# Cross-attention on one core: joins of the maxima ahead of the block maxima, K out behind the scores, and two products moved to GpSimd

## The chip, the core and the metric

The kernel runs on one core of one Trainium2 chip. A core has five engines that run their own queues in order and wait for each other by semaphores: PE (TensorE, matrix products, results into PSUM banks), ACT (ScalarE), DVE (VectorE), POOL (GpSimd, no access to PSUM) and SP (SyncE, which issues most DMAs here). The metric is the device time of one execution in microseconds (us); lower is better.

## What is computed

Layer norm of a context, multi-head cross-attention over it, an output projection with a gate and a residual, for 32 batches of 112 queries and 375 context rows, 512 features, 16 heads of 32, all in float32:

```python
a = _layer_norm(audio_kv, ln_gamma, ln_beta)
Q = (hidden_states @ Wq.T).reshape(B, Tt, HEADS, HEAD_DIM).transpose(0, 2, 1, 3)
K = (a @ Wk.T).reshape(B, Ta, HEADS, HEAD_DIM).transpose(0, 2, 1, 3)
V = (a @ Wv.T).reshape(B, Ta, HEADS, HEAD_DIM).transpose(0, 2, 1, 3)
scores = jnp.einsum('bhtd,bhsd->bhts', Q, K) * scale
scores = jnp.where(mask, scores, jnp.float32(-jnp.inf))
attn = jax.nn.softmax(scores, axis=-1)
out = jnp.einsum('bhts,bhsd->bhtd', attn, V)
out = out.transpose(0, 2, 1, 3).reshape(B, Tt, D)
out = out @ Wo.T
return hidden_states + jnp.tanh(gate) * out
```

## The kernel before

**Split products.** Each large product is made of three passes: both factors are split into a high part, which TensorE's fast float32 format holds exactly, and a low part (the rest), and high·high, high·low and low·high are added. So for each tensor there is a high half (a copy into that format, on ACT for the context and the attention output) and a low half (a subtraction of the high half).

**Stages.** In the first 92 us the weights are prepared, all of Q is computed (L960) and kept in DRAM. Then the main loop runs over 64 slot pairs m. A slot, or chunk, p is a group of four heads of one batch: 4 per batch, 128 in all. Slot pair m belongs to batch c = m // 2 and is even or odd. In what follows "slot" with a number up to 63 means such a pair.

**PE in slot m.** K projection of chunk 2m, a V part (or, in odd slots from batch 3 on, the output product of batch c − 3 as the fourth product), K projection of chunk 2m+1, another of these; the weighted sums of chunks 2m−6 and 2m−5 (L1093) with their denominators (L1099); and the scores of chunks 2m and 2m+1 (L1080). K projections all use bank KB = 6, as do the weighted sums; V and outputs use bank 7. The scores of a chunk have three parts j of 125 context rows. The two chunks of a slot share banks 0 to 5: parts 0 and 1 of the even chunk lie in banks 0 to 3, part 2 begins in banks 4 and 5.

**The maxima.** After ACT has moved the scores to `prob` (L608, scaled, with the mask as bias), DVE takes block maxima over 32 rows by transposing reductions (L833, `quadrant_maxima`), three for each chunk. They are in four partition quarters; SP stores them to DRAM and loads them back so that each partition has all of them (`exchange_maxima`, L361 and L368, into `x4` for even chunks, `x_odd` for odd ones). One slot later DVE joins them (L821, into `top`), spreads the result over the columns of PSUM bank 0 (L824, `spread`), and subtracts it from the scores (L843, three times). ACT takes the exponential (L617), POOL adds the three parts of a chunk (L475, L479, `sum_chunks`), and the denominators are made of these sums. In the last but one pair the spread maxima lie in SBUF, in `rspread`, instead of the bank.

**Normalising and output.** ACT moves the weighted sums and denominators out (L658, `weighted_out`). Once per batch, in even slots, DVE reduces the denominators, takes the reciprocal, spreads it into `rspread` and multiplies (`normalise`, L848 to L858). In the odd slot behind it ACT makes the high half (L634), DVE the low half (L862). PE multiplies by Wo one batch later, ACT moves this out with the gate (L640, `gated`), POOL adds the input with its bias (L461, L467), SP stores.

**What sets the order.** Every engine's queue is written by hand in a function `slot_pair(m)` of its own, and what follows the loop stands behind it. The last batch is drained separately: the weighted sums of chunks 122, 124 and then 126 and 127, outputs 29, 30 and the last, which is split into quarters (`last_divide`, `last_low`, `last_output`). The semaphores named in the change are `sub_done` (subtractions), `o_norm` (a batch is normalised), `o_hi` and `o_done` (its high and low halves), `rspread_done` and `top_done`.

## Time and profile before

| what | value |
|---|---|
| median of 3 runs | 960.72 us (960.67 to 962.39) |
| the profiled execution | 958.61 us |
| its span, first to last instruction | 956.8 us |
| mean granted TensorE clock | 0.996 |
| PE busy | 932.9 us, 97% |
| DVE busy | 810.9 us, 85% |
| ACT busy | 689.6 us, 72% |
| POOL busy | 589.6 us, 62% |

The page is read from the busy shares to the waits: an engine that is busy throughout sets the pace, and idle time of the others costs nothing unless it ends in a wait of that engine. Busy times are those of instructions as the profiler records them; the ends of matmuls are modelled. A row of a timeline shows instructions of one kind merged; the bracket at its end is the idle time of that engine before them and what ended it.

### The profile page before, as it was taken

The page shows a single profiled execution, that of the slowest core. Times are in us where ns is not written, and L with a number is a line of the kernel's source. Part 1 is how long each engine was busy: PE and PEld are TensorE (multiplying, and loading weights), DVE is VectorE, ACT ScalarE, POOL GpSimd, SP SyncE. Part 2 cuts the span into 40 slices and gives each one's busy share as a digit, 9 for nine tenths or more (in the row PEclk, how much of TensorE's full clock was granted, in tenths as well). Part 3 has the DMA queues.
Part 4 walks back from the last instruction along what each step waited for, and adds up shares of the span by engine and source line. Part 5 has one row for each costly group of instructions (what it writes and reads, how often), then busy time and mean ns, then how long its engine had stood idle before and what let it go on. Part 6 is the DMA issues. An engine that isn't in the chain of part 4 may idle for free.

```text
span 956.8 us, 26687 instructions
## 1 busy us (share of the span) xinstructions
PE 932.9 (97%) x10687; PEld 807.7 (84%) x10687; DVE 810.9 (85%) x1446; ACT 689.6 (72%) x1299; POOL 589.6 (62%) x665
## 2 busy tenths in 40 slices
PE   8999988999999999999999999999999999999967
PEld 8889877888888888888888888888888888888854
DVE  6873379898888899889988888898889988888896
ACT  2422677777877778777778787778777778777773
POOL 0851356666666667766667666667676667666554
PEclk9999999999999999999999999999999999999999
DMA  9974133324443333444344444334444344433101
GB/s 284 348 223 166 28 94 93 93 70 108 108 113 101 97 93 98 110 112 106 95 98 112 110 105 105 85 94 113 109 112 109 80 110 109 113 94 99 38 21 58
DMA packets 85852, 105.54 MB, mean 110 GB/s; under 512 B 22529, under 2 KB 63489, under 8 KB 85729
## 3 DMA queue, kind: packets, MB, share of 16 engines
q1 hardware_dynamic: 85152, 102.93, 40.5%
q8 instruction: 84, 1.38, 0.6%
q10 hardware_dynamic: 576, 0.92, 0.3%
q14 instruction: 40, 0.32, 0.1%
HBM read 86.39 MB, written 17.43 MB: 109 GB/s over the span
## 4 chain that ended last, share of the span: by engine, by line
PE 88%; DVE 6%; DMA 2%; POOL 1%; ACT 1%; issue 1%; SPq 0%; DVEq 0%; ACTq 0%; POOLq 0%
PE banks L937 62%; PE banks L1080 10%; PE banks L1093 8%; PE banks L960 5%; PE banks L1099 2%; DVE shared_q L843 2%; DMA shared_q<-in_wvT 2%; DVE rmax L833 1%; DVE banks L824 1%; POOL gbo L445 1%; POOL xy L449 1%; ACT shared_q L608 1%; DMA shared_q<-in_wqT 0%; DVE top L821 0%; DVE wq L737 0%
## 5 line engine op out<-in xcount | busy, mean ns | idle before, releaser
L937 PE MATMUL banks<-shared_r,w_k 128*128 128x376 f32 x1536 | 291.7, 339 | 0.0
L937 PE MATMUL banks<-w_v,shared_r 128*125 128x512 f32 x1152 | 284.4, 396 | 0.0
L937 PEld LDWEIGHTS banks<-shared_r,w_k 128*128 128x128 f32 x1536 | 263.1, 188 | 12.9
L475 POOL TENSOR_TENSOR shared_f<-shared_q 125x448 f32<-125x448 f32 x126 | 146.9, 1166 | 199.6 <-PE banks L1099 198.4
L833 DVE TRANSPOSE_TENSOR_REDUCE rmax<-shared_q 128x14 f32<-128x448 f32 x384 | 220.6, 620 | 55.5 <-ACT shared_q L608 55.4
L608 ACT ACTIVATE shared_q<-banks,maskT,rstd 125x448 f32<-125x448 f32 x384 | 249.9, 726 | 4.8 <-PE banks L1080 4.8
L937 PEld LDWEIGHTS banks<-w_v,shared_r 128*125 128x125 f32 x1152 | 213.2, 186 | 45.2 <-issue 0.2
L843 DVE TENSOR_TENSOR shared_q<-shared_q,banks 125x448 f32<-125x448 f32 x378 | 212.0, 616 | 4.4
L617 ACT ACTIVATE shared_q<-shared_q 125x448 f32<-125x448 f32 x384 | 193.1, 569 | 5.9 <-DVE shared_q L843 5.8
L479 POOL TENSOR_TENSOR shared_f<-shared_f,shared_q 125x448 f32<-125x448 f32 x126 | 154.0, 1222 | 9.9
L455 POOL TENSOR_TENSOR shared_r<-cn,shared_r 128x375 fp32r<-128x375 f32 x124 | 111.9, 923 | 75.1 <-ACT shared_r L564 75.0
L628 ACT ACTIVATE shared_f<-banks,rstd 125x512 f32<-125x512 f32 x96 | 66.2, 689 | 60.5 <-PE banks L937 60.5
L1080 PE MATMUL banks<-shared_q,shared_f 32*125 32x112 f32 x3072 | 101.5, 276 | 6.4 <-DVE shared_q L843 6.4
L1080 PEld LDWEIGHTS banks<-shared_q,shared_f 32*125 32x125 f32 x3072 | 90.2, 184 | 18.0 <-issue 18.0
L1093 PEld LDWEIGHTS banks<-shared_q,shared_f 125*32 125x32 f32 x3072 | 72.4, 110 | 32.3 <-issue 23.1
L1093 PE MATMUL banks<-shared_q,shared_f 125*32 125x112 f32 x3072 | 89.0, 263 | 8.0 <-ACT shared_q L608 5.4
L937 PE MATMUL banks<-w_o,shared_r 128*112 128x512 f32 x372 | 91.9, 396 | 0.1
L622 ACT ACTIVATE shared_f<-banks 128x376 f32<-128x376 f32 x128 | 62.3, 487 | 40.9 <-PE banks L937 40.9
L824 DVE STREAM_TRANSPOSE banks<-top 128x448 f32<-128x448 f32 x126 | 83.1, 660 | 4.3
L960 PE MATMUL banks<-shared_r,wq 128*128 128x448 f32 x384 | 82.6, 377 | 0.7 <-ACT wq L546 0.7
L960 PEld LDWEIGHTS banks<-shared_r,wq 128*128 128x128 f32 x384 | 73.6, 192 | 9.1 <-issue 1.0
L937 PEld LDWEIGHTS banks<-w_o,shared_r 128*112 128x112 f32 x372 | 64.5, 174 | 19.0 <-DVE shared_r L862 0.3
(94 smaller groups left out, 742.9 us busy)
## 6 DMA issues: line engine op xcount, KB each, us to landing
cn<-in_ctxT SPq DMA_DIRECT2D x128, 187.5 KB, 3.7
rows<-in_ctx SPq DMA_DIRECT2D x32, 720.0 KB
xy<-in_x SPq DMA_DIRECT2D x32, 224.0 KB, 7.3
q_kept<-shared_q SPq DMA_DIRECT2D x8, 896.0 KB, 5.4
shared_q<-q_kept SPq DMA_DIRECT2D x32, 224.0 KB, 4.3
out<-xy SPq DMA_DIRECT2D x32, 224.0 KB, 3.6
shared_f<-in_xT SPq DMA_DIRECT2D x7, 896.0 KB, 11.0
x<-row_stats SPq DMA_DIRECT2D x64, 84.0 KB
```

Of the source, the lines that this page charges most:

```text
L455: pool.tensor_tensor(cT[:, p, 1, k, 0:S], cn[:, m % (2 * KT), :], cT[:, p, 0, k, 0:S].bitcast(F32), ALU.subtract) \
L475: pool.tensor_tensor(psum[0:SP_, h, :], prob[0:SP_, q, 0, :], prob[0:SP_, q, 1, :], ALU.add).then_inc(sum_half, 1)
L479: pool.tensor_tensor(psum[0:SP_, h, :], psum[0:SP_, h, :], prob[0:SP_, q, 2, :], ALU.add).then_inc(sum_done, 1)
L608: act.activation(prob[0:SP_, n % NB, j, :] .rearrange("p (a h t) -> p a h t", a=2, h=2), score_view(n, j), ACT.Identity, bias=maskT[0:SP_, ...
L617: act.activation(prob[0:SP_, n % NB, j, :], prob[0:SP_, n % NB, j, :], ACT.Exp, scale=SCALE).then_inc(exp_done, 1)
L824: dve.transpose(maxima_of(p).rearrange("p (k a) -> p k a", a=32), top[:, :].unsqueeze(2).to_broadcast([128, BLK, 32])) \
L833: last = dve.tensor_reduce(rmax[:, n % 2, BLK * j:BLK * j + BLK], prob[:, n % NB, j, :].rearrange("p (k a) -> p k a", a=32), AX.X, ALU.max ...
L843: dve.tensor_tensor(prob[0:SP_, p % NB, j, :], prob[0:SP_, p % NB, j, :], maxima_of(p)[0:SP_, :], ALU.subtract).then_inc(sub_done, 1)
L937: last = pe.matmul(dst, l, m, start=(start and k == 0), stop=(stop and k == len(pairs) - 1))
L960: return pe.matmul(q_bank(g, m)[:, 0:GN], wq[:, a, k, 128 * m:128 * m + 128], xr[:, g, c, k, :], start=(k == 0 and e == 0), stop=(k == KT ...
L1080: last = pe.matmul(bank[banks[h]][0:SP_, T * places[h]:T * places[h] + T], kT[part, n % 2, SP_ * j:SP_ * j + SP_], qT[part, c % QB, u, :], ...
L1093: pe.matmul(dst[HD * h:HD * h + HD, :], v_sb[0:SP_, c % VB, j, col:col + HD], prob[0:SP_, p % NB, j, T * h:T * h + T], start=(j == 0), sto ...
```

## The change

- `join_maxima`: the joins of the chunks of slot m−1 are made ahead of the block maxima of slot m, both of them, into a `top` of two halves; then, behind the block maxima, come two spreads and six subtractions.
- The spread maxima lie in bank 4 and bank 5 (even and odd chunk), for the last two chunks in bank 0. PE's wait for the subtractions stands ahead of part 2 of the even chunk's scores instead of ahead of part 0.
- ACT: K out of the even chunk (`k_out(2m+2)`) comes behind both score evictions; the exponential of the odd chunk (`exponential(2m−3)`) ahead of `weighted_out`.
- The product by the reciprocal (`normalised`) and the low half (`low_half`) are POOL's. In the loop they stand behind the sums of the slot, the product in even slots and the low half in odd ones; for batch 30 both stand behind the loop, ahead of the sums of chunks 124 and 125.
- DVE waits for `o_norm` before it writes `rspread` again.

```diff
-        top = sb("top", [128, BLK])
+        top = sb("top", [128, 2, BLK])
...
@@ gpsimd
+            def normalised(b):
+                pool.wait_ge(rspread_done, b + 1)
+                o = pv[:, b % 2 * HT:b % 2 * HT + HT]
+                pool.tensor_tensor(o, o, rspread[:, :], ALU.mult).then_inc(o_norm, 1)
+
+            def low_half(b):
+                pool.wait_ge(o_hi, b + 1)
+                pool.tensor_tensor(oT[:, 1, :, :].rearrange("p c t -> p (c t)"),
+                                   pv[:, b % 2 * HT:b % 2 * HT + HT],
+                                   oT[:, 0, :, :].rearrange("p c t -> p (c t)").bitcast(F32),
+                                   ALU.subtract).then_inc(o_done, 1)
...
                 if pair(m - 2):
                     sum_chunks(2 * m - 4)
                     sum_chunks(2 * m - 3)
+                if odd and c > 1:
+                    low_half(c - 2)
                 if not odd and m >= 0:
+                    if c > 1:
+                        normalised(c - 2)
...
             for m in range(-1, PAIRS):
                 slot_pair(m)
+            normalised(B - 2)
+            low_half(B - 2)
             add_bias(B - 3)
             sum_chunks(SLOTS - KT)
             sum_chunks(SLOTS - KT + 1)
@@ scalar, slot_pair
+                if pair(m - 2):
+                    exponential(2 * m - 3)
                 if pair(m - 3):
                     weighted_out(2 * m - 6)
-                if pair(m - 2):
-                    exponential(2 * m - 3)
...
                 if pair(m):
                     scores_out(2 * m)
-                if pair(m + 1):
-                    k_out(2 * m + 2)
...
                 if pair(m):
                     scores_out(2 * m + 1)
                 if pair(m + 1):
+                    k_out(2 * m + 2)
                     first_out(m + 1)
@@ vector
-                return rspread[:, :] if p // 2 == PAIRS - 2 else spread
+                if p // 2 == PAIRS - 2:
+                    return rspread[:, :]
+                return bank[0 if p // 2 == PAIRS - 1 else 4 + p % 2][:, 0:HT]
...
+                need(dve, o_norm, b)
                 dve.transpose(rspread[:, :].rearrange("p (k a) -> p k a", a=32),
...
-                dve.wait_ge(rspread_done, b + 1)
-                o = pv[:, b % 2 * HT:b % 2 * HT + HT]
-                dve.tensor_tensor(o, o, rspread[:, :], ALU.mult).then_inc(o_norm, 1)
...
+                if pair(m - 1):
+                    join_maxima(2 * m - 2)
+                    join_maxima(2 * m - 1)
                 if m == PAIRS - 1:
+                    dve.wait_ge(o_norm, B - 2)
                     without_maximum(SLOTS - 4)
                     without_maximum(SLOTS - 3)
                 quadrant_maxima(2 * m)
                 quadrant_maxima(2 * m + 1)
                 if pair(m - 1) and m < PAIRS - 1:
-                    without_maximum(2 * m - 2)
-                    without_maximum(2 * m - 1)
+                    spread_maximum(2 * m - 2)
+                    spread_maximum(2 * m - 1)
+                    subtract_maximum(2 * m - 2)
+                    subtract_maximum(2 * m - 1)
@@ tensor, scores
                     need(pe, s_out, n * ST)
-                    need(pe, sub_done, (n - 2) * ST)
                 for j in range(ST):
                     banks, places = score_place(n, j)
+                    if n % 2 == 0 and j == 2:
+                        need(pe, sub_done, (n - 2) * ST)
```

In the rows below a line number of the changed kernel differs from that of the kernel before; the names tell them apart. VectorE (DVE) in an even slot and the start of the odd one, before:

```order
L858 TENSOR_TENSOR shared_f<-shared_f,rspread 128x448 [waits rspread_done]
L833 TENSOR_REDUCE rmax<-shared_q 128x14 [waits s_out,max_stored]
L833 TENSOR_REDUCE rmax<-shared_q 128x14 [waits s_out] x2
L833 TENSOR_REDUCE rmax<-shared_q 128x14 [waits s_out,max_stored]
L833 TENSOR_REDUCE rmax<-shared_q 128x14 [waits s_out] x2
L821 TENSOR_REDUCE top<-x_49 128x14 [waits ld_max0]
L824 STREAM_TRANSPOSE banks<-top 128x448 [waits top_done]
L843 TENSOR_TENSOR shared_q<-shared_q,banks 125x448 [waits spread_done]
L843 TENSOR_TENSOR shared_q<-shared_q,banks 125x448 x2
L821 TENSOR_REDUCE top<-x_odd 128x14 [waits ld_max1]
L824 STREAM_TRANSPOSE banks<-top 128x448 [waits top_done]
```

The same engine after, from the joins on:

```order
L839 TENSOR_REDUCE top<-x_49 128x14 [waits ld_max0]
L839 TENSOR_REDUCE top<-x_odd 128x14 [waits ld_max1]
L853 TENSOR_REDUCE rmax<-shared_q 128x14 [waits s_out,max_stored]
L853 TENSOR_REDUCE rmax<-shared_q 128x14 [waits s_out] x2
L853 TENSOR_REDUCE rmax<-shared_q 128x14 [waits s_out,max_stored]
L853 TENSOR_REDUCE rmax<-shared_q 128x14 [waits s_out] x2
L844 STREAM_TRANSPOSE banks<-top 128x448 [waits top_done] x2
L863 TENSOR_TENSOR shared_q<-shared_q,banks 125x448 [waits spread_done]
```

The two joins (of `x4`, printed `x_49`, and `x_odd`) have moved ahead of the six block maxima, and the product by `rspread` is gone. ScalarE (ACT) in an odd slot, from the gated eviction of the output to K out, before:

```order
L640 ACTIVATE gated<-banks,gat 112x512 [waits y_done,y_mm]
L634 ACTIVATE shared_r<-shared_f 128x448 [waits y_mm,o_norm]
L658 ACTIVATE shared_f<-banks 128x2x224 [waits dsum_done,o_done,pv_mm]
L617 ACTIVATE shared_q<-shared_q 125x448 [waits sub_done] x3
L608 ACTIVATE shared_q<-banks,maskT,rstd 125x448 [waits s_mm]
L608 ACTIVATE shared_q<-banks,maskT,rstd 125x448 x2
L622 ACTIVATE shared_f<-banks 128x376 [waits k_mm]
L608 ACTIVATE shared_q<-banks,maskT,rstd 125x448 [waits s_mm]
L608 ACTIVATE shared_q<-banks,maskT,rstd 125x448 x2
```

The same after:

```order
L657 ACTIVATE gated<-banks,gat 112x512 [waits y_done,y_mm]
L651 ACTIVATE shared_r<-shared_f 128x448 [waits y_mm,o_norm]
L634 ACTIVATE shared_q<-shared_q 125x448 [waits sub_done] x3
L675 ACTIVATE shared_f<-banks 128x2x224 [waits dsum_done,o_done,pv_mm]
L625 ACTIVATE shared_q<-banks,maskT,rstd 125x448 [waits s_mm]
L625 ACTIVATE shared_q<-banks,maskT,rstd 125x448 x2
L625 ACTIVATE shared_q<-banks,maskT,rstd 125x448 [waits s_mm]
L625 ACTIVATE shared_q<-banks,maskT,rstd 125x448 x2
L639 ACTIVATE shared_f<-banks 128x376 [waits k_mm]
```

The exponentials now stand ahead of the eviction of the weighted sums, and K out behind the six score evictions. GpSimd (POOL) at the end of the kernel, from `result(28)` to the end, before:

```order
L467 TENSOR_TENSOR xy<-xy,gated 112x512 [waits y_out,xb_done]
L461 TENSOR_TENSOR xy<-xy,gbo 112x512 [waits ld_x1]
L475 TENSOR_TENSOR shared_f<-shared_q 125x448 [waits pv_mm,exp_done]
L479 TENSOR_TENSOR shared_f<-shared_f,shared_q 125x448 [waits exp_done,sum_half]
L475 TENSOR_TENSOR shared_f<-shared_q 125x448 [waits pv_mm,exp_done]
L479 TENSOR_TENSOR shared_f<-shared_f,shared_q 125x448 [waits exp_done,sum_half]
L467 TENSOR_TENSOR xy<-xy,gated 112x512 [waits y_out,xb_done]
```

The same after:

```order
L466 TENSOR_TENSOR xy<-xy,gated 112x512 [waits y_out,xb_done]
L472 TENSOR_TENSOR shared_f<-shared_f,rspread 128x448 [waits rspread_done]
L476 TENSOR_TENSOR shared_r<-shared_f,shared_r 128x448 [waits o_hi]
L460 TENSOR_TENSOR xy<-xy,gbo 112x512 [waits ld_x1]
L486 TENSOR_TENSOR shared_f<-shared_q 125x448 [waits pv_mm,exp_done]
L490 TENSOR_TENSOR shared_f<-shared_f,shared_q 125x448 [waits exp_done,sum_half]
L486 TENSOR_TENSOR shared_f<-shared_q 125x448 [waits pv_mm,exp_done]
L490 TENSOR_TENSOR shared_f<-shared_f,shared_q 125x448 [waits exp_done,sum_half]
```

The product and the low half of batch 30 (L472, L476) now stand ahead of the bias addition and the sums of chunks 124 and 125.

## Rows read from the trace of the kernel before

**Rows 1.** the page: the span, and TensorE's busy tenths in 40 slices of it
```profile
span 956.8 us, 26687 instructions
...
PE   8999988999999999999999999999999999999967
```

**Rows 2.** waits of PE: operation, releaser, us in total, times, longest us
```profile
PE banks L1080 <- DVE shared_q L843: 6.4, 4, 1.9
```

**Rows 3.** timeline of PE, first slots: start us, us, line, operation, count, [idle before]
```profile
123.46 1.58 PE L1080 MATMUL banks<-shared_q,shared_f 32*125 32x112 f32 x48 [1.06 <-DVE shared_q L843]
...
162.00 1.58 PE L1080 MATMUL banks<-shared_q,shared_f 32*125 32x112 f32 x48 [1.87 <-DVE shared_q L843]
```

**Rows 4.** timeline of SP (DMA issues), same columns: one early, two late
```profile
112.62 0.53 SPq L368 DMA_DIRECT2D x_odd<-row_stats  x1
...
916.42 0.53 SPq L361 DMA_DIRECT2D row_stats<-rmax  x1
919.48 0.52 SPq L368 DMA_DIRECT2D x_odd<-row_stats  x1
```

**Rows 5.** timeline of DVE, a steady pair of slots: product and low half
```profile
413.06 1.61 DVE L858 TENSOR_TENSOR shared_f<-shared_f,rspread 128x448 f32<-128x448 f32 x1
...
423.36 0.63 DVE L862 TENSOR_TENSOR shared_r<-shared_f,shared_r 128x448 fp32r<-128x448 f32 x1
```

**Rows 6.** timeline of ACT, one steady odd slot
```profile
422.18 0.69 ACT L640 ACTIVATE gated<-banks,gat 112x512 f32<-112x512 f32 x1 [0.91 <-PE banks L937]
422.76 0.57 ACT L634 ACTIVATE shared_r<-shared_f 128x448 fp32r<-128x448 f32 x1
423.93 0.54 ACT L658 ACTIVATE shared_f<-banks 128x448 f32<-128x448 f32 x1 [0.59 <-issue]
424.37 1.50 ACT L617 ACTIVATE shared_q<-shared_q 125x448 f32<-125x448 f32 x3
425.77 1.95 ACT L608 ACTIVATE shared_q<-banks,maskT,rstd 125x448 f32<-125x448 f32 x3
```

**Rows 7.** timeline of PE, end of the kernel
```profile
932.32 2.47 PE L1093 MATMUL banks<-shared_q,shared_f 125*32 125x112 f32 x48 [5.39 <-ACT shared_q L608]
...
935.40 3.05 PE L937 MATMUL banks<-w_o,shared_r 128*112 128x512 f32 x12
...
940.84 3.04 PE L937 MATMUL banks<-w_o,shared_r 128*112 128x512 f32 x12
```

**Rows 8.** timeline of PE, the odd slot of rows 6
```profile
422.07 1.36 PE L1093 MATMUL banks<-shared_q,shared_f 125*32 125x112 f32 x48
...
423.74 1.58 PE L1080 MATMUL banks<-shared_q,shared_f 32*125 32x112 f32 x48
425.25 0.96 PE L937 MATMUL banks<-shared_r,w_k 128*128 128x376 f32 x4
```

**Rows 9.** timeline of POOL, the first sum of that slot
```profile
423.80 1.19 POOL L475 TENSOR_TENSOR shared_f<-shared_q 125x448 f32<-125x448 f32 x1 [2.69 <-PE banks L1099]
```

**Rows 10.** timeline of DVE, end of the kernel
```profile
922.82 3.74 DVE L843 TENSOR_TENSOR shared_q<-shared_q,rspread 125x448 f32<-125x448 f32 x3
...
937.14 0.65 DVE L853 STREAM_TRANSPOSE rspread<-rden 128x448 f32<-128x448 f32 x1
...
948.83 0.28 DVE L883 TENSOR_TENSOR shared_r<-shared_f,shared_r 128x112 fp32r<-128x112 f32 x1 [0.17 <-ACT shared_r L645]
949.02 0.85 DVE L876 RECIPROCAL shared_f<-banks 128x112 f32<-128x112 f32 x1
...
953.32 0.75 DVE L891 SCALAR_TENSOR_TENSOR xy<-banks,gat,xy 112x512 f32<-112x512 f32 x1 [0.79 <-PE banks L1061]
```

**Rows 11.** timeline of POOL, end of the kernel
```profile
935.33 1.15 POOL L475 TENSOR_TENSOR shared_f<-shared_q 125x448 f32<-125x448 f32 x1 [7.63 <-PE banks L1099]
```

**Rows 12.** windows: busy us (x) of PE, PEld, DVE, ACT, POOL, PEclk, DMA share, GB/s
```profile
932.00:934.00 2.00, 1.69 (x37) 1.69 (x41) 0.94 (x2) 0.84 (x2) 0.00 (x0) 0.50 0.11 23
```

**Rows 13.** waits of PEld, PE's weight loads, in the columns of rows 2
```profile
PEld banks L1080 <- issue: 18.0, 64, 2.1
```

23 lines of the change are left out of this document (9 added, 14 removed).

## The prediction

> **What bounds the kernel now.** I read the page first: TensorE is at nine tenths or full in every slice except the first ones and the last two of a span of 956.8 us [rows 1]. So in the loop nothing that another engine gives up can shorten the time; only PE's idle places and the drain at the end can move it. I then read the waits of PE. The wait of the score matmuls for the subtraction of the maxima comes only four times, 6.4 us in all [rows 2]. Three of the four are in the first slots, the first 1.06 and the third 1.87 us [rows 3]; with 1.54 for the one between (the total less the other three, to the rounding) they are 4.47; the fourth (1.89) is in the last slot, and there PE soon runs into a longer wait anyway. Once the loop is in step the score matmuls follow the weighted sums with no wait. Last I read the timelines of all engines for one steady pair of slots and for the last 50 us, since the change reorders every queue.
>
> **Start of the loop.** The spread maxima of slots m−1 leave bank 0, so scores of slot m wait for the subtraction only ahead of their third part, which begins about a third into 1.5 us, some 0.5 us later. The joins lie ahead of the block maxima, so some 0.8 us (estimate: two operations shorter than 0.5 each) leave VectorE's queue behind the last of these. The second and third stall (1.54 and 1.87) need about 2 us, and these two steps together with the earlier start of ScalarE's score evictions (K out no longer stands between them, about 0.4 us) cover them: I take both as gone. The first one is doubtful. The odd join now stands ahead of the block maxima, and its load is issued at 112.62 [rows 4]. No row shows a load's landing; the nearest is a store's round trip, from 916.42 to 919.48, 3.06 us with its issue [rows 4]. So the join cannot start before about 115.7. Behind it come six block maxima, two spreads and six subtractions, 14 operations of 448 columns, each at most the 0.63 us of an uncontended one [rows 5]; at 0.57 in a row they end near 123.7 at the latest value of the landing and 123.3 at one 0.4 earlier, and the third part of the scores wants them near 122.9 (123.46 − 1.06 + 0.5). About 0.6 of 1.06 stays. Gain at the start: 4.47 − 0.6 = **3.9 us** (3.2 to 4.5).
>
> **The steady slots.** VectorE gives up the product and the low half; GpSimd takes them. PE's sequence of work is the same, and its own time is what a slot costs. What I have to ask is whether a new wait appears. K out behind all scores: six score evictions, 1.95 us for three with the overlap of a next one [rows 6], take 3.7 us from the end of the scores, and K out less than 0.5. PE's second K projection of the next slot, which needs it, begins some 4.9 us after the end of the scores, behind two products (3.04 us for one of 512 columns, three quarters of that for one of 376 [rows 7]; less what overlaps): 0.6 us to spare. Weighted sums out behind the exponential is tight. In an odd slot PE starts the weighted sums at 422.07 and needs their bank for the next K projection at 425.25 [rows 8]. ScalarE starts the gated eviction at 422.18, the high half 0.58 us later, then another 0.47, then three exponentials that free it after 1.40, then the eviction of 0.54 [rows 6]. 422.18 + 0.58 + 0.47 + 1.40 + 0.54 = 425.17, where it was 423.93 + 0.54 = 424.47. That leaves 0.08 us for a semaphore's hop from ScalarE to PE. The one hop that these rows show, from PE's output product (its successor starts at 422.07) to ScalarE at 422.18, is 0.11 us. So the wait is between nothing (a hop inside the slack) and 0.1 us, in 28 odd slots: 0 to 2.8 us. I take the difference to the hop shown, 0.02 to 0.03 us each, **0.6 us**. The next score evictions, queued behind it on ScalarE, start when the scores end, near 425.4, and are not moved.
>
> GpSimd: the product lasted 1.61 us on VectorE while GpSimd was summing, the low half 0.63 while it was idle [rows 5]; on GpSimd each is priced as its own 448-column sum, 1.15 to 1.19, and before the next sums it sat idle for 2.69 us in that slot [rows 9]. One added operation in each slot fits, so in the loop they cost nothing. The low half is ready some 6 us later, and PE wants it a whole pair of slots on. If that cover were gone each slot would cost up to 1.2 us.
>
> Here the Trainium skill speaks against the move: GPSIMD Engine Reference, section "Engine selection", says to keep elementwise work with two inputs on VectorE because GpSimd is about twice as slow. The uncontended rows agree (1.15 against 0.63). The contended product does not bear it out, 1.61 against 1.15, and by the page's factor of about two on 0.63 the two operations would take 2.5 us together instead of my 2.3; that would add 0.2 us to the drain below and nothing in the loop.
>
> **The drain.** Here the two operations are on the path. The last slot's maxima first: load of the odd maxima was issued at 919.48 [rows 4]. The block maxima end about 0.5 us earlier than before, so the load starts near 919.0, and lands (again by the store's round trip) near 921.7. The join now stands ahead of the even slot's subtraction, so spread and subtraction start near 922.4 to 922.8, where the subtraction started at 922.82 [rows 10]; it runs beside GpSimd's sums as before (3.74 us for three). From there the exponentials and evictions run in the order they had. The fourth stall is thus covered by this chain. Call S the start of the next weighted sums, 932.32 before [rows 7]; I take S = **931.9** (931.1 to 932.4).
>
> Before, from S to the end of VectorE's last operation were 953.32 + 0.75 − 932.32 = 21.75 us [rows 7, 10]. After, follow GpSimd's queue. The spread reciprocal ends at 937.79, S + 5.48 [rows 10], unchanged. GpSimd then has, in this order, the product (to S + 6.7), the low half, which waits for ScalarE's high half (from S + 7.4 to S + 8.55), a bias addition (1.3, by its 512 columns against 448), and only then the four sums for the chunk pair 124 and 125. These started at 935.33, S + 3.0, before [rows 11]; now at S + 9.85. Four of them at 1.15 to 1.19 end at S + 14.6. PE is in order: the denominators of that pair wait, behind them the output product of batch 30, which started at 940.84, S + 8.5 [rows 7], and now starts at S + 15.1. So PE has idled some 7 us but for eight small matmuls. After the 5.39 us idle time the granted clock was 0.50, the level of 1.2 GHz [rows 12], and the work from 932.32 to 935.40 [rows 7] took 3.08 us where the same took 1.67 in the loop [rows 8]. So I charge 1.5 us (0 to 2.1, the whole product at half speed) on 3.05: output 30 ends at S + 19.6.
>
> Behind it everything is serial. ScalarE evicts it (0.62) and only then takes the last three exponentials (1.40) [rows 6], the first high quarter (0.3, as a low one) and VectorE two low quarters (0.28 each, overlapping) [rows 10]: so the third reciprocal starts 2.8 us after output 30. From there to the end were 954.07 − 949.02 = 5.05 us [rows 10], with nothing to shorten them. The end is S + 19.6 + 2.8 + 5.05 = S + 27.4 = 959.3 against 954.07. What the freed VectorE gains (its last subtraction ends some 3.5 us earlier) waits for GpSimd. Drain: **+5.2 us** (+3.1 with a warm clock and S at 931.4, +6.4 with a fully cold product and S at 932.3).
>
> **The sum.** −3.9 + 0.6 + 5.2 = +1.9 us on a span of 956.8. The profiled execution took 958.6 and the median of the runs is 960.7; I add the difference to the median: **962.6 us**, which is 0.2% slower. About 0.2%, 1.9 us, is also what a measurement of this kernel can tell from no change.
>
> **Rivals.**
> (A) ScalarE's margin is gone: the exponential ahead of the eviction makes the K projection wait 0.1 us or more in each odd slot. For it: 0.08 us of slack in [rows 6, 8]. Against: the hop may fit. It decides as soon as hop and jitter exceed 0.08 us. Price 0.1 × 28 = 2.8 instead of 0.6: **964.8**, slower. Chance 0.19.
> (B) A shorter head of the scores, the other side: PE's weight loads sit idle before the 64 score blocks, 18.0 us in all with no releaser [rows 13], and one of its three waits moves to the third part, where it is hidden by running matmuls. If 0.06 us of that is the wait itself, 64 slots give −3.8: **958.8**, faster. Against: the same number of waits is issued, the moved one in the middle of a block of short matmuls. Chance 0.13.
> (C) The drain costs less: warm clock, early load, and all three stalls gone: −4.5 + 0 + 3.1 = −1.4, **959.3**; for it only that three uncertain terms all lie at their good end. Chance 0.08. That the order isn't what it seems is no case: GpSimd's queue has the low half ahead of the sums.
>
> **Chances and range.** My forecast holds 0.60, over 960.4 to 964.2; 0.36 of it within 0.2% of 960.7, 0.24 slower. (A) gives 0.17 slower, 0.02 same; (B) 0.10 faster, 0.03 same; (C) 0.05 faster, 0.03 same. Faster 0.15, same 0.44, slower 0.41. The range goes from 959.1, inside (B) and (C), to 965.6, beyond (A).
>
> **What would show it.** No wait of score matmuls for subtractions after slot 5, and at most one short one before. On GpSimd the four last sums start near 10 us after S. PE idles twice in the drain for GpSimd's sum, then shows a clock of 0.50. The last three exponentials follow the eviction of output 30. In odd slots the K projection's wait for ScalarE is 0 to 0.1 us. I am wrong if those last sums start at S + 3, if PE waits in steady slots for anything longer, or if the slots get shorter or longer without a wait.

## The result and the profile after

The changed kernel takes **966.87 us** (median of 4 runs, 964.51 to 969.5) against 960.69 for the kernel before in the same comparison (959.33 to 962.39): a ratio of 1.0068, with a 95% interval of 1.005 to 1.0086. It is slower by some 6 us. I had forecast 962.6, in a range of 959.1 to 965.6, so the prediction was wrong. It charged the drain and missed a ring through the exchange of the maxima: a chain of waits that leads from the load of one slot's maxima to the load of the next slot's, and so has to fit into one slot.

The page of the kernel after, with its span, TensorE's busy tenths and the engines' shares of the chain that ended last; it answers to [rows 1]:

```profile
span 967.7 us, 26688 instructions
...
PE   8999999999999999999999999999999999999955
...
PE 61%; DMA 22%; DVE 7%; ACT 4%; issue 2%; POOL 2%; SPq 1%; DVEq 0%; ACTq 0%; POOLq 0%
```

The tenths tell little: two early slices are fuller than before, the last two emptier. The last line tells more: 22% of the chain is DMA, in a kernel whose PE is "full" in every slice of the loop. The same line before:

```profile
PE 88%; DVE 6%; DMA 2%; POOL 1%; ACT 1%; issue 1%; SPq 0%; DVEq 0%; ACTq 0%; POOLq 0%
```

Next, PE's waits in the kernel after (operation, releaser, us in total, times, longest), which answer to [rows 2]:

```profile
PE banks L1112 <- ACT shared_q L625: 9.5, 1, 9.5
PE banks L1118 <- POOL shared_f L490: 6.4, 2, 4.7
PE banks L955 <- ACT shared_f L675: 2.0, 6, 0.4
...
PE banks L1099 <- DVE shared_q L863: 1.7, 2, 1.1
```

The first two are in the drain, the third is a K projection that waits for ScalarE's eviction of the weighted sums, the fourth is what is left of the waits for subtractions. VectorE's waits, same columns:

```profile
DVE top L839 <- DMA x_odd<-row_stats: 131.4, 54, 4.1
```

The join of the odd maxima waits for its load in 54 of 64 slots, 131.4 us in all. None of these waits is there before.

**Stages.** For each kernel I cut the profiled execution at starts that all have, and give the length of each stage in us. "Start" runs from the first K projection (after the preparation) to the 10th slot's scores, "loop" from there to those of the 63rd (53 slots), "last" from there to S, the start of the weighted sums of chunk 122, and "drain" to the end of VectorE's last operation. The last column is the median of all timed runs.

| kernel | start | loop | last | drain | sum | median |
|---|---|---|---|---|---|---|
| before | 122.53 | 693.60 | 24.37 | 21.75 | 862.25 | 960.69 |
| after | 121.17 | 696.01 | 24.98 | 28.06 | 870.22 | 966.87 |
| e1_joins_behind | 118.67 | 694.13 | 22.98 | 28.47 | 864.25 | 959.74 |
| e2_last_on_dve | 120.39 | 696.10 | 26.22 | 22.95 | 865.66 | 961.44 |
| e3_act_order_back | 121.42 | 693.59 | 24.99 | 28.04 | 868.04 | 964.02 |
| e4_behind_and_last | 118.68 | 694.13 | 24.05 | 21.85 | 858.71 | 955.19 |
| e5_also_act_back | 118.30 | 693.59 | 24.16 | 22.95 | 859.00 | 955.10 |
| e6_even_join_ahead | 118.53 | 694.68 | 22.80 | 28.41 | 864.42 | 960.12 |
| e7_products_on_dve | 122.65 | 698.36 | 25.70 | 21.75 | 868.46 | 960.71 |
| e8_only_move | 122.20 | 693.60 | 23.64 | 27.49 | 866.93 | 963.60 |
| e9_ring_shorter | 119.04 | 694.55 | 23.62 | 28.68 | 865.89 | 961.57 |
| e10_ring_longer | 119.86 | 694.64 | 25.12 | 28.60 | 868.22 | 963.72 |

The preparation, whose code is the same everywhere, ended between 90.2 and 94.7 us in these executions, so it is left out of the stages. After is 8.0 us longer by the stages: start −1.4, loop +2.4, last +0.6, drain +6.3. The medians differ by 6.2; the profiled execution of before is 2.1 under its median and that of after 2.6 over, of which the preparation explains 2.9. The other 1.8 of the 8.0 belong to these two executions and not to the kernels.

How far one execution can be trusted shows in e2 (below), which has the code of after up to S: its loop agrees to 0.1 us, its start differs by 0.8 and its last stage by 1.2. So small differences of the loop can be read from one execution, those of the start and the last stage only when they are larger than about 1 us.

### The profile page after: what moved, and what is told of

Same layout as the page of the kernel before. It is cut to its first block, busy times and chain, and to the rows that moved or that the text cites. A ratio compares the mean times of both kernels' runs of the same rounds, so it can differ in the third digit from the quotient of the medians.

```text
span 967.7 us, 26688 instructions
## 1 busy us (share of the span) xinstructions
PE 937.1 (97%) x10687; PEld 809.8 (84%) x10687; DVE 705.1 (73%) x1384; ACT 692.4 (72%) x1299; POOL 646.5 (67%) x727
## 4 chain that ended last, share of the span: by engine, by line
PE 61%; DMA 22%; DVE 7%; ACT 4%; issue 2%; POOL 2%; SPq 1%; DVEq 0%; ACTq 0%; POOLq 0%
PE banks L955 42%; DMA row_stats<-rmax 13%; DMA x_odd<-row_stats 8%; PE banks L1099 6%; PE banks L1112 5%; PE banks L978 5%; DVE rmax L853 5%; DMA shared_q<-in_wvT 2%; PE banks L1118 2%; ACT shared_q L634 2%; ACT shared_q L625 2%; SPq L367 1%; POOL gbo L444 1%; POOL xy L448 1%; DVE shared_q L863 1%
## 5 line engine op out<-in xcount | busy, mean ns | idle before, releaser
L625 ACT ACTIVATE shared_q<-banks,maskT,rstd 125x448 f32<-125x448 f32 x384 | 243.4, 728 | 23.8 <-PE banks L1099 23.8
L486 POOL TENSOR_TENSOR shared_f<-shared_q 125x448 f32<-125x448 f32 x126 | 144.6, 1148 | 169.5 <-ACT shared_q L634 110.9
L853 DVE TRANSPOSE_TENSOR_REDUCE rmax<-shared_q 128x14 f32<-128x448 f32 x384 | 209.8, 610 | 17.4 <-ACT shared_q L625 17.4
L634 ACT ACTIVATE shared_q<-shared_q 125x448 f32<-125x448 f32 x384 | 197.4, 570 | 31.6 <-DVE shared_q L863 31.2
L863 DVE TENSOR_TENSOR shared_q<-shared_q,banks 125x448 f32<-125x448 f32 x378 | 204.9, 606 | 0.1
L490 POOL TENSOR_TENSOR shared_f<-shared_f,shared_q 125x448 f32<-125x448 f32 x126 | 144.6, 1148 | 9.9
L839 DVE TENSOR_REDUCE top<-x_odd 128x14 f32<-128x168 f32 x64 | 29.2, 456 | 131.6 <-DMA x_odd<-row_stats 131.4
L955 PE MATMUL banks<-w_o,shared_r 128*112 128x512 f32 x372 | 94.2, 403 | 0.0
```

The lines of the kernel that those rows point to most:

```text
L486: pool.tensor_tensor(psum[0:SP_, h, :], prob[0:SP_, q, 0, :], prob[0:SP_, q, 1, :], ALU.add).then_inc(sum_half, 1)
L490: pool.tensor_tensor(psum[0:SP_, h, :], psum[0:SP_, h, :], prob[0:SP_, q, 2, :], ALU.add).then_inc(sum_done, 1)
L625: act.activation(prob[0:SP_, n % NB, j, :] .rearrange("p (a h t) -> p a h t", a=2, h=2), score_view(n, j), ACT.Identity, bias=maskT[0:SP_, ...
L634: act.activation(prob[0:SP_, n % NB, j, :], prob[0:SP_, n % NB, j, :], ACT.Exp, scale=SCALE).then_inc(exp_done, 1)
L853: last = dve.tensor_reduce(rmax[:, n % 2, BLK * j:BLK * j + BLK], prob[:, n % NB, j, :].rearrange("p (k a) -> p k a", a=32), AX.X, ALU.max ...
L863: dve.tensor_tensor(prob[0:SP_, p % NB, j, :], prob[0:SP_, p % NB, j, :], maxima_of(p)[0:SP_, :], ALU.subtract).then_inc(sub_done, 1)
```

## The ring, in the trace of after

SyncE's timeline over two slots and a half (start us, us to issue, line, transfer):

```profile
558.89 0.52 SPq L367 DMA_DIRECT2D x_odd<-row_stats  x1
...
564.78 0.53 SPq L360 DMA_DIRECT2D row_stats<-rmax  x1
566.91 0.54 SPq L367 DMA_DIRECT2D x<-row_stats  x1
567.55 0.53 SPq L360 DMA_DIRECT2D row_stats<-rmax  x1
570.85 0.52 SPq L367 DMA_DIRECT2D x_odd<-row_stats  x1
571.42 0.94 SPq L275 DMA_DIRECT2D cn<-in_ctxT  x2
572.41 0.83 SPq L281 DMA_DIRECT2D rows<-in_ctx  x2
...
576.86 0.54 SPq L360 DMA_DIRECT2D row_stats<-rmax  x1
580.93 0.55 SPq L367 DMA_DIRECT2D x<-row_stats  x1
...
584.89 0.52 SPq L367 DMA_DIRECT2D x_odd<-row_stats  x1
```

The ring is: load of the odd maxima, join, three block maxima of the next even chunk, store, load, store, load of the odd maxima. A turn has to fit into one slot because the join stands ahead of the block maxima. Before, the block maxima of slot m stood ahead of the join of slot m−1's maxima, so a turn had two slots, and no join ever waited for a load. One turn, added up from 558.89: landing 3.73 us (the join starts at 562.64), 0.40 until the first block maximum (563.02), 1.70 for three of them with 0.06 to the store at 564.78, its round trip 2.13, 0.64 to the second store, 3.30 until the odd load: 11.96. The next turn is 14.04, since the store at 576.86 stands behind the loads of contexts, rows and input of a new batch: its round trip is 4.07. Together that is 26.00 us, where PE's work for two slots takes 26.18 (2 × 13.09). So the ring has next to no slack against PE, and some turns are longer: over the loop the store behind these loads took 2.1 to 5.3 us, in the median of 27 of them 4.5. What happens when it is late shows in the chain that ended last (start us, us, what):

```profile
558.89 3.73 DMA x_odd<-row_stats
...
563.02 3.27 DVE rmax L853 x6
566.28 1.07 DVE banks L844 x2
...
567.89 1.63 ACT shared_q L634 x3
...
571.50 0.44 ACT shared_f L675
...
572.08 9.95 PE banks L955 x48
```

and in PE's timeline:

```profile
572.08 2.30 PE L955 MATMUL banks<-shared_r,w_k 128*128 128x376 f32 x12 [0.37 <-ACT shared_f L675]
```

The load lands at 562.62, the block maxima, spreads and subtractions follow, ScalarE's exponential waits for these, the eviction of the weighted sums (L675) stands behind the exponential in its queue, and PE's K projection waits for the bank: 0.37 us, in a slot of 13.65 us. Four slots of the loop go over 13.14 in this way (13.34, 13.65, 13.43, 13.48), with such a wait of 0.21 to 0.37 us in each. For these waits two parts of the change are needed: the joins ahead, and the exponential ahead of the eviction (e3).

## The experiments

**e1: the joins behind the block maxima again.** In the last pair each join stands right ahead of its own spread.

```diff
-                if pair(m - 1):
-                    join_maxima(2 * m - 2)
-                    join_maxima(2 * m - 1)
                 if m == PAIRS - 1:
...
                 if pair(m - 1) and m < PAIRS - 1:
+                    join_maxima(2 * m - 2)
+                    join_maxima(2 * m - 1)
                     spread_maximum(2 * m - 2)
```

> The changed kernel with one part undone: both joins of the maxima stand behind the block maxima again (the spreads, the two banks, the queues of ScalarE and GpSimd stay as changed). Theory R (ring): with the joins ahead, VectorE waits for the odd maxima's load (131 us in 64 waits), and block maxima, store, load, store, load, join form a ring of some 12 to 13.5 us that sometimes exceeds PE's 13.09 us per slot. Then this run has almost no waits of joins for loads, the first slots gain 4.0 to 4.5 us against the kernel before instead of 1.4, no slot is longer than 13.13, and the time is 3 to 4 us under the changed kernel: near 963.5. Rival (the lost time in the loop is ScalarE's order or GpSimd's load): the same slots stay long, time near 966.9.

Measured: 959.74 us (958.56 to 960.64), 0.9992 of before (0.9976 to 1.0007). VectorE's wait is gone:

```profile
DVE top L839 <- DMA x_odd<-row_stats: 0.3, 1, 0.3
```

This is 7.1 us less than after, twice what I expected even of this theory. The stages show why: the ring costs not in one place but in three, 2.5 us at the start, 1.9 in the loop, 2.0 in the last stage.

**e2: product and low half of batch 30 on VectorE.** The loop is as in the change.

```diff
@@ gpsimd
-            normalised(B - 2)
-            low_half(B - 2)
             add_bias(B - 3)
@@ vector
             normalise(B - 2)
+            dve.wait_ge(o_norm, B - 2)
+            normalised_here(B - 2)
+            dve.wait_ge(o_done, B - 2)
+            low_half_here(B - 2)
             join_maxima(SLOTS - 2)
```

> The changed kernel with only batch 30's product and low half (behind the loop) back on VectorE; all other batches stay on GpSimd. Theory Q (queue in the drain): they stand ahead of the last four sums on GpSimd and PE waits 6.4 us for these. Then the sums start 3 us after the weighted sums of chunk 122, PE waits for GpSimd under 1 us, and from those weighted sums to the last VectorE operation it is 21.5 to 22 us instead of 28.1: 6 us less, near 961. Rival (the drain is long because PE ran cold and the load of the odd maxima came late): under 2 us less.

Measured: 961.44 us (958.79 to 963.07), 1.0018 (1.0003 to 1.0033). The time is as expected; the drain is 5.1 us shorter (22.95, where I had said 21.5 to 22), 5.4 by the medians. The 1 us too much is taken up under e5.

**e3: ScalarE's eviction of the weighted sums ahead of the exponential, as before.**

```diff
                 if pair(m - 3):
                     weighted_out(2 * m - 6)
+                if pair(m - 2):
+                    exponential(2 * m - 3)
```

(and the exponential ahead of it is gone)

> The changed kernel with ScalarE's exponentials behind the eviction of the weighted sums again. Theory M (ScalarE's margin): the 0.02 to 0.04 us by which odd slots exceed 13.09 and the 0.35 us waits of the K projection for this eviction come from that order; they go, and the time falls by 1 to 2 us, near 965.5. Rival (they come from the ring or from GpSimd): odd slots stay at 13.12, time near 966.9.

Measured: 964.02 us (963.54 to 965.12), 1.0051 (1.0033 to 1.0068): 2.9 us under after, more than the 1.4 expected. By the stages the gain, 2.4, is all in the loop, which is back at 693.59 although the joins still wait for their loads:

```profile
DVE top L839 <- DMA x_odd<-row_stats: 87.9, 35, 4.0
```

ScalarE then absorbs the lateness: the eviction goes first, and PE does not wait for it. With the joins behind and the exponential ahead (e1, e4) the loop takes 694.13. So the exponential alone costs 0.54 us, the joins alone nothing that the loop shows, both together 2.4. The start and the last stage are not helped by this order.

**e4: e1 and e2 together.** The two edits above.

> The first two edits together: joins behind the block maxima, batch 30's product and low half on VectorE. If ring and queue are separate causes, their gains add: 9 to 10 us under the changed kernel, near 957.5, which is 3 us under the kernel before. If one hides the other, near 961.

Measured: 955.19 us (953.97 to 955.67), 0.9955 (0.9942 to 0.9968), better than both kernels and 2.3 under what I expected. The gains of e1 and e2 over after, 7.1 and 5.4, nearly add up: 11.7. So ring and queue are separate causes. PE's end of it (start, us, count, idle before):

```profile
928.45 2.47 PE L1127 MATMUL banks<-shared_q,shared_f 125*32 125x112 f32 x48 [8.57 <-ACT shared_q L623]
...
931.60 3.48 PE L970 MATMUL banks<-w_o,shared_r 128*112 128x512 f32 x12
...
937.06 3.05 PE L970 MATMUL banks<-w_o,shared_r 128*112 128x512 f32 x12 [0.16 <-DVE shared_r L883]
```

Output 30 starts at S + 8.6, as it did before (S + 8.5, [rows 7]), and at full speed.

**e5: e4 and e3 together.**

> The run with joins behind and batch 30 on VectorE, and ScalarE's exponentials behind the eviction of the weighted sums as well. Theory M: that order alone made odd slots 13.11 instead of 13.09 (28 of them, 0.5 us) and made the K projection wait about 0.35 us twice at the start, so this run is 0.5 to 1.3 us under that one: near 954.2, and beats both kernels by over half a per cent. Rival: with the joins behind, the later exponentials delay something else and it is not faster than 955.2.

Measured: 955.10 us (953.61 to 956.29), 0.9943 (0.9928 to 0.9958). The loop gives back the 0.54 us and the start 0.4, but the drain is 1.1 longer, so against e4 nothing is decided. The traces tell where the 1.1 are. Output 29 took 3.91 us against 3.48 in e4, because the granted clock stayed at 0.50 until S + 5 instead of S + 4; and VectorE's low half, which began after an addition of GpSimd had begun, took 1.33 instead of 0.63:

```profile
934.57 1.33 DVE L883 TENSOR_TENSOR shared_r<-shared_f,shared_r 128x448 fp32r<-128x448 f32 x1 [1.38 <-ACT shared_r L649]
```

In e2 the same two are 3.75 and 1.49. K out behind the scores and PE's moved wait were never taken back alone; e5 has both, and its loop is that of before.

**e6: the even join ahead, only the odd one behind.**

```diff
                 if pair(m - 1):
                     join_maxima(2 * m - 2)
-                    join_maxima(2 * m - 1)
...
+                    join_maxima(2 * m - 1)
                     spread_maximum(2 * m - 2)
```

> The changed kernel with only the odd join moved back behind the block maxima; the even join stays ahead. Theory R says the ring closes through the last load of a slot, that of the odd maxima: without it VectorE waits almost nothing for loads, all slots are 13.09 to 13.13, and the time is within 1 us of the run with both joins behind (959.7). Rival: any join ahead closes the ring through its own load; then waits for the even load take the place of the others and the time stays above 963.

Measured: 960.12 us (958.61 to 962.93), 0.9999 (0.9987 to 1.0012), within 0.4 of e1. The even load is issued some 4 us earlier and is in time, so the ring closes through the odd load alone, and an even join ahead costs no more than the 0.55 us by which this loop is longer than e1's.

**e7: all products and low halves on VectorE, the rest of the change kept.**

```diff
@@ gpsimd: normalised and low_half taken out, loop and drain
@@ vector, normalise
                     .then_inc(rspread_done, 1)
+                normalised_here(b)
@@ vector, slot_pair
+                if odd and c > 1:
+                    low_half_here(c - 2)
```

> The changed kernel with product and low half of all batches on VectorE again. If the move to GpSimd is worth something only in the drain, where it costs 6 us, the rest of this kernel is as good or better without it: near 961, as with batch 30 alone moved back. If VectorE's 2.2 us in a pair of slots lengthen the ring (the product stands ahead of the joins in even slots), slots get longer than 13.13 in numbers and the time is over 963.

Measured: 960.71 us (960.01 to 964.81), 1.0011 (0.9998 to 1.0024). The drain is 21.75, exactly before's. The loop is 698.36, the longest but for e11 and e12, with nine slots of 13.26 to 14.06, as the second theory wanted; but the time is where the first one put it. The profiled execution was 2.9 us over e7's median, so its stages stand too high by up to that. By the medians e7 is no slower than e2 (961.44), which differs from it only in that the operations of the other batches are on GpSimd. So the 2.4 us by which this one loop is longer than that of after are not shown to be the move's: whether GpSimd gains anything in the loop stays open. In the drain the move costs 6.3 us (28.06 against 21.75).

**e8: the kernel before with nothing but the move to GpSimd** (functions and places as in the change, with the waits for `o_norm`).

> The kernel before with one part alone: product and low half on GpSimd for all batches, joins, bank 0 and ScalarE's order as before. Theory Q prices it: 5.5 to 6 us more in the drain, in the loop a gain of 0.5 to 1.5 us in the first slots (VectorE is done earlier), so 4 to 5.5 us above the kernel before: near 964.5. Rival (the drain is long for another part of the change): within 1.5 us of the kernel before.

Measured: 963.60 us (962.5 to 967.25), 1.0039 (1.0025 to 1.0053). The loop is before's 693.60 to the hundredth, so GpSimd's place there costs nothing, as predicted; the drain is 5.74 longer, start and last stage together 1.1 shorter. The medians of this comparison differ by 3.4 (963.60 against 960.24), somewhat under the 4 to 5.5 expected and well over the rival's 1.5. PE's wait for the late sums is the same as in after:

```profile
PE banks L1106 <- POOL shared_f L491: 6.4, 2, 4.7
```

**e9: a shorter ring.** SyncE stores both chunks' maxima, waits once and loads both; the block maxima of a pair wait for the stores of the pair ahead.

```diff
-                    (store 2m, wait, load 2m, store 2m+1, wait, load 2m+1)
+                store_maxima(2 * m)
+                store_maxima(2 * m + 1)
+                sync.wait_ge(max_stored, 32 * (m + 1))
+                load_maxima(2 * m)
+                load_maxima(2 * m + 1)
```

> The changed kernel with the exchange alone in another order on SyncE: both stores of a slot, one wait for both, both loads. The odd maxima's store then starts when its block maxima are done instead of behind the even chunk's round trip, which takes 1 to 1.5 us out of the ring. Theory R: the waits of joins for loads fall from 131 us by 1 us or more for each odd slot, no slot is longer than 13.13, the first nine slots get 1 to 2 us shorter than 121.2, the slots of the loop take about 694.2 as with the joins behind, and the time falls by 2.5 to 4 us, near 963.5. Rival (the long slots come from something else than this exchange): no change.

Measured: 961.57 us (960.46 to 963.9), 1.0017 (1.0005 to 1.0028), 5.3 us under after with the joins still ahead. The waits:

```profile
DVE top L843 <- DMA x_odd<-row_stats: 13.0, 28, 1.1
```

A tenth of this waiting is left, no slot is over 13.13, and the run brings some three quarters of what e1 does. The gain is more than expected, and lies in the same three stages.

**e10: a longer ring, as I meant it.** The loads of the contexts are issued between the odd chunk's store and its load.

```diff
                 store_maxima(2 * m + 1)
+                for n in (2 * m + 8, 2 * m + 9):
+                    if n < SLOTS:
+                        load_ctx(sync, n)
                 sync.wait_ge(max_stored, 16 * (2 * m + 2))
                 load_maxima(2 * m + 1)
```

(and the same loop behind it is gone)

> The changed kernel with the two loads of the context issued ahead of the load of the odd maxima instead of behind it: that load lands later by up to 1 us, behind 190 KB each, and nothing else is moved. Theory R: the ring, 12 to 13.5 us, now exceeds 13.09 in many slots, and the 53 slots of the loop take 5 to 40 us more than 696: time 971 to 1005. Rival (the ring has slack in nearly all slots, and the joins' wait for loads is a wait that costs nothing): within 1 us of the changed kernel.

Measured: 963.72 us (962.65 to 964.85), 1.0036 (1.0023 to 1.0049). A miss: I expected 971 at least, and it is 3 us faster than after. SyncE's timeline shows the error:

```profile
547.51 0.53 SPq L359 DMA_DIRECT2D row_stats<-rmax  x1
548.09 0.94 SPq L275 DMA_DIRECT2D cn<-in_ctxT  x2
550.78 0.54 SPq L368 DMA_DIRECT2D x_odd<-row_stats  x1
```

The two issues fit inside the store's round trip (3.27 us, no longer than without them), so they delay nothing; and the contexts are under way some 3 us earlier and farther from the next even store, whose trip in odd slots fell from 4.5 us to 2.2 in the median. The waits of the join fell to 58.0 us in 33 slots. The edit shortened the ring where I had meant to lengthen it, so its gain speaks for the ring and not against it.

**e11: one more trip in the ring.** The odd chunk's maxima are stored a first time, and SyncE waits for this before it stores them as usual.

```diff
                 sync.wait_ge(quad_max, p + 1)
+                if q:
+                    sync.dma_start(..., rmax[:, q, :]).then_inc(again, 16)
+                    sync.wait_ge(again, 16 * (p // 2 + 1))
```

> The changed kernel with each store of the odd maxima made twice, the second when the first has landed, so that the exchange is longer by one round trip, 2 to 3 us by the stores in the traces; nothing else is changed. Theory R: with the joins ahead the exchange is in a ring of some 12 to 12.5 us, which becomes 14 to 15.5 us, above PE's 13.09; the 54 slots of the loop take 50 to 130 us more than 696: 1020 to 1095 us in all. Rival (the waits of joins for loads have slack that costs nothing, and the long slots are something else): within 3 us of 966.9.

Measured: 1099.21 us, 1.1457 (1.1417 to 1.1497), slightly above the upper end. The loop's mean slot is 15.29 us. Not all of the increase is the trip: PE waits so often that its granted clock fell to 0.50 in stretches of the loop (0.949 over the whole run, 0.991 in e12). The chain that ended last, one turn:

```profile
527.69 1.69 DVE rmax L860 x3
...
529.45 4.21 DMA row_stats<-rmax
...
534.31 3.07 DMA row_stats<-rmax
...
537.39 2.10 DMA row_stats<-rmax
...
539.51 3.73 DMA x_odd<-row_stats
```

**e12: the same extra trip with the joins behind, as in e1.** By the ring alone it should have cost nothing.

> The same doubled store in the run with the joins behind the block maxima (959.7 us). Theory R: there the exchange has the time of the block maxima and of the wait for the scores in addition, some 4 us of slack in each slot, so an additional 2 to 3 us cost nothing in the loop and at most their own length in the last slot: 959.7 to 963. If it costs as much as in the other kernel, the place of the joins is not what matters.

Measured: 1034.32 us, 1.0781 (1.0749 to 1.0812), slots of 14.36 us. A miss, of 70 us. Even with the joins behind, VectorE waits for loads (96.0 us in 63 slots) and for stores to be done with `rmax` (76.7 us), because SyncE issues one exchange after the other and its queue is now full:

```profile
525.84 0.52 SPq L367 DMA_DIRECT2D row_stats<-rmax  x1
533.29 0.55 SPq L374 DMA_DIRECT2D x<-row_stats  x1
...
539.03 0.54 SPq L374 DMA_DIRECT2D x_odd<-row_stats  x1
```

From odd load to odd load (522.95 to 539.03) are 16.08 us here, 7.45 of them one store behind the context loads. I had reckoned with 4 us to spare in this queue. The extra trip takes some 3 us and the slots grew by 1.27, so less than 2 us a slot were free. The same extra trip costs 0.9 us a slot more when the joins stand ahead (15.29 against 14.36), part of it by e11's lower clock. As a test of the ring the pair is weak: the ring is shown by e1, e6 and e9.

## Why the prediction was wrong, point by point

**The start: a gain of 3.9 us.** The mechanism was right, and e1 realises it: 122.53 − 118.67 = 3.86 us. In the change only 1.4 is left (e2, with the same code, has 2.1). PE's timeline of after answers to [rows 3]:

```profile
127.07 1.14 PE L1099 MATMUL banks<-shared_q,shared_f 32*125 32x112 f32 x32 [1.12 <-DVE shared_q L863]
...
138.89 1.14 PE L1099 MATMUL banks<-shared_q,shared_f 32*125 32x112 f32 x32 [0.62 <-DVE shared_q L863]
```

I had kept 0.6 of the first stall and taken the second as gone; they are 1.12 and 0.62. VectorE's first odd join ended its wait at 119.15, 3.39 us after its load was issued (115.76); the next load, issued at 127.04, took 3.91. I had priced the landing by a store's round trip, 3.06 [rows 4], and in this first slot only; that the second slot's chain begins with the second load, I left out. Two K projections of the start wait for ScalarE's eviction as well, 0.38 and 0.35 us, which I had not looked for here.

**The steady slots: +0.6 for ScalarE's margin.** This term was right. Every other slot is 13.11 to 13.13 us long where it was 13.09, and the loop of e1 and e4 is 0.53 longer than before's. Rival A, at 0.1 us a slot, did not occur; nor did B: the loop of e5, without either wait, is 693.59 against 693.60 before, so the moved wait gains nothing.

**The step that failed** is the one behind "What I have to ask is whether a new wait appears": the sum puts the join's wait for its load at nothing in the steady slots. I asked the question of K out, of the weighted sums out and of GpSimd, and not of the join, the one instruction that I had just found waiting for a DMA at the start. The runs showed 131.4 us of such waits in 54 slots. With my own 3.06 us of [rows 4] for the landing and for each store's trip, and the pieces between as the trace of after has them, a turn adds up to 3.06 + 0.40 + 1.76 + 3.06 + 0.64 + 3.06 = 12.0 us against 13.09: near enough for a rival of its own. I had drawn it as a delay within one slot, which the slot's idle time covers, and not as a ring, which has to fit in every turn. It costs 1.9 us in the loop, 2.5 at the start and 2.0 at the end (e1 against after), 7.1 us by the medians. The prediction's own sign of being wrong, a longer wait of PE in steady slots, came up four times (0.21 to 0.37 us).

**S.** I took 0.4 us less for the way to S; it is 0.6 more. The last ring turn decides: VectorE's timeline shows the odd join of the last pair (bracket: idle before, releaser).

```profile
926.41 0.45 DVE L839 TENSOR_REDUCE top<-x_odd 128x14 f32<-128x168 f32 x1 [3.45 <-DMA x_odd<-row_stats]
```

Its load was issued at 922.64 and landed 3.75 later, not 3.06. The prediction also added wrongly here: 919.0 + 3.06 is 922.1 and not 921.7, which alone takes back the 0.4 us. With the joins behind (e1) the last stage is 2.0 shorter than in after, and 1.4 under before.

**The drain: +5.65 us from S on.** The mechanism was right and the size 0.7 short: 6.31. GpSimd's end:

```profile
945.28 1.13 POOL L476 TENSOR_TENSOR shared_r<-shared_f,shared_r 128x448 fp32r<-128x448 f32 x1 [1.63 <-ACT shared_r L651]
946.36 1.27 POOL L460 TENSOR_TENSOR xy<-xy,gbo 112x512 f32<-112x512 f32 x1
947.59 1.12 POOL L486 TENSOR_TENSOR shared_f<-shared_q 125x448 f32<-125x448 f32 x1
...
951.08 1.13 POOL L490 TENSOR_TENSOR shared_f<-shared_f,shared_q 125x448 f32<-125x448 f32 x1
```

S is 936.89; the sums start at S + 10.70 where I said 9.85 ([rows 11] had them at S + 3.0), and end at S + 15.3. PE waits for them as foretold:

```profile
940.04 3.97 PE L955 MATMUL banks<-w_o,shared_r 128*112 128x512 f32 x12
...
949.97 0.60 PE L1118 MATMUL banks<-shared_f,ones 125*32 125x112 f32 x8 [4.67 <-POOL shared_f L490]
...
952.79 4.38 PE L955 MATMUL banks<-w_o,shared_r 128*112 128x512 f32 x12
```

Output 30 starts at S + 15.9 (15.1) and takes 4.38 (4.55, that is 3.05 and 1.5 for the clock). The granted clock, in the columns of [rows 12], around output 29 and around output 30:

```profile
939.00:941.00 2.00, 2.00 (x26) 1.46 (x19) 0.19 (x1) 0.54 (x1) 0.00 (x0) 0.50 0.19 50
941.00:943.00 2.00, 2.00 (x8) 1.49 (x7) 1.90 (x5) 0.00 (x0) 0.51 (x1) 0.73 0.26 21
...
952.00:954.00 2.00, 1.74 (x11) 1.17 (x12) 0.44 (x1) 1.02 (x3) 2.00 (x3) 0.50 0.04 8
```

For output 30, 0.50 is the level of 1.2 GHz, after PE had idled for 4.67 us, as it was after 5.39 before. The missing 0.7 us is in one step. Output 29, which starts at S + 3.15, took 3.97 us where it had taken 3.05 [rows 7]; ScalarE evicts it ahead of the high half, and so the low half started at S + 8.39 where I had S + 7.4. Output 29 was slower because the clock, at 0.50 after PE had idled for 9.50 us ahead of S (5.39 before), was back at full speed only about S + 5. Before, it was back by S + 3, when output 29 began:

```profile
934.00:936.00 2.00, 2.00 (x39) 1.60 (x29) 0.00 (x0) 0.39 (x1) 0.67 (x1) 0.68 0.20 54
```

When the clock comes back differs between executions, and no run shows what sets it: e7 had idled for 9.37 us, and its output 29 took 3.05. In the runs with the sums behind the two operations, output 29 took 3.04 to 4.39 us and output 30 4.1 to 5.5. So the charge of 1.5 us for the clock is 1.3 here by luck; the others show 1.1 to 2.4, beyond the upper end of 2.1 that I had given it. That end was not worked out either: by 3.08 against 1.67 us, a whole product at the lower level takes 2.6 us more. The ends of the drain's range, added up again, are +3.3 and +6.3 instead of +3.1 and +6.4.

On the price of GpSimd's operations: product and low half take 1.16 and 1.13 there, 2.3 us together as estimated, and in e4 on VectorE 1.36 and 0.63. The Trainium skill's GPSIMD Engine Reference, section "Engine selection", with its factor of about two, fits the low half (1.8) and not the contended product (0.85). In the drain neither decides; that two operations stand ahead of four sums on one engine does.

**The sum.** Start +2.5 missed, loop +1.8, way to S +1.0, drain +0.7: 6.0 us between the forecast (+1.9) and the stages (+8.0); by the medians 4.3 us are missing (966.87 against 962.6). The first three are the ring.

## What to carry to other kernels

When an instruction that waits for a DMA is moved ahead of the work that feeds that same DMA, follow the loop once round and add it up, landing included, for each kind of slot: every turn starts where the last one ended, so its length has to stay under the pace of the bounding engine. A busy share of nine tenths in every slice doesn't show it; the chain that ended last (DMA 22%) and the other engines' waits do. And count the issuing queue too: e12 has no such ring within one slot, and still one more awaited store in SyncE's queue made each slot 1.3 us longer. And where a loop hides an operation on a lightly loaded engine, the drain may not: the same move that is free in e8's loop costs 5 to 6 us of the last 30 by the stages, 3.4 (e8) and 5.4 (e2) by the medians. e4 keeps it in the loop alone, and is 0.5% faster than the kernel before.

## What the runs showed of the hardware

- A small store to DRAM and back to its semaphore took 2.1 us in quiet stretches of after, 2.8 to 3.5 as the second of two, and in the median 4.5 (up to 5.3) some 3.5 us behind the issue of bulk loads on the same queue (576.86: 4.07). In e12, where it mostly follows the loads at once, it took 7.5 in the median (525.84: 7.45). The Trainium skill, DMA: Bandwidth & Descriptors, section "Latency and other measured facts", gives HBM access as slower at high load. The trace agrees in direction, by a factor of two to three and a half on the whole trip; no run here separates the memory's part from that of the queue.
- The loads of the odd maxima released their waiter 3.1 to 4.2 us after they were issued in after, longer than the quiet store (2.1); the load writes 84 KB, each row to several partitions, the store 21 KB.
- Three subtractions that read `rspread` in SBUF took 3.5 to 4.8 us where GpSimd worked throughout; with GpSimd idle three such took 1.70 (931.86 in after), and three that read a PSUM bank took 1.68 beside GpSimd's work (918.99 in before). Of the second three, e4's took 4.64 and e1's 3.57, and e4's last stage is 1.1 us over e1's.
- The preparation, the same code in all kernels, took from 90.2 to 94.7 us. The loop stage tells differences of 0.5 us in one execution (693.59 to 693.60 in before, e3, e5 and e8), whole executions don't.
